# A gated attention and MLP block on one core: another order of the prelude

## The reference

```python
x = x + tanh(g_xattn[0]) * wkv(time_decay, time_first, layernorm(x), ctx)
x = x + tanh(g_ffn[0]) * ffn(layernorm(x), W1, W2, W3)

# ffn: D = 512, H = 2048
hidden = silu(x @ W1.T) * (x @ W3.T)
hidden = fwht(hidden)                 # orthonormal Walsh-Hadamard over H
out = hidden @ W2.T
```

## Time and profile before

| | |
|---|---|
| Median of three runs | 1129.24 us (1128.84 to 1130.64) |
| The profiled execution's own time | 1130.67 us |
| Its span, first to last instruction | 1128.8 us |
| PE busy | 1074.0 us, 95% of the span |
| DVE, ACT, POOL busy | 586.9, 305.3, 291.2 us |
| Mean granted clock of PE | 0.982 |

### The profile page before, as it was taken

One profiled execution on the slowest core, in us unless ns is written; L12 is line 12 of the kernel. 1 busy time (PEld: TensorE's weight loads), 2 busy tenths in 40 slices (PEclk: granted clock), 3 DMA queues, 4 the chain that ended last, 5 costly groups with the idle time before them and its releaser, 6 DMA issues.

```text
span 1128.8 us, 12951 instructions
## 1 busy us (share of the span) xinstructions
PE 1074.0 (95%) x4878; PEld 504.0 (45%) x4972; DVE 586.9 (52%) x849; ACT 305.3 (27%) x373; POOL 291.2 (26%) x194
## 2 busy tenths in 40 slices
PE   5677999799999999999999999999999999999998
PEld 2235444344444444444444444444444444444443
DVE  7744686537527555556527454556537464541112
ACT  5634542132312330231312330141412330110000
POOL 0121115212431134213431134213341225211111
PEclk9787999999999999999999999999999999999999
DMA  9924103000120012000120011000120000000001
GB/s 344 355 71 146 60 1 112 0 38 1 38 75 1 38 38 75 1 40 1 38 75 1 38 38 75 1 39 1 38 75 1 38 1 1 1 19 19 1 1 38
DMA packets 20387, 55.65 MB, mean 49 GB/s; under 512 B 1504, under 2 KB 10848, under 8 KB 17504
## 3 DMA queue, kind: packets, MB, share of 16 engines
q1 hardware_dynamic: 20320, 54.73, 13.6%
HBM read 42.14 MB, written 12.58 MB: 48 GB/s over the span
## 4 chain that ended last, share of the span: by engine, by line
PE 92%; ACT 3%; DVE 3%; issue 2%; DMA 1%; SPq 0%; DVEq 0%; ACTq 0%
PE pg L478 10%; PE pl L478 10%; PE po L486 10%; PE pg L476 10%; PE pl L476 10%; PE po L484 9%; PE pl L477 9%; PE pg L477 9%; PE po L485 9%; PE po L459 2%; PE po L452 1%; PE pst L411 1%; DMA w3h<-w_t 1%; ACT w L655 1%; PE pst L447 1%
## 5 line engine op out<-in xcount | busy, mean ns | idle before, releaser
L1053 POOL TENSOR_TENSOR work<-work 128x512 bf16<-128x512 f32 (+1 forms) x132 | 204.9, 1552 | 710.9 <-DVE work L903 710.9
L896 DVE TENSOR_TENSOR work<-work,pl 128x512 f32<-128x512 f32 (+1 forms) x132 | 88.3, 669 | 459.3 <-PE pl L478 446.3
L636 ACT ACTIVATE work<-pg 128x512 f32<-128x512 f32 (+1 forms) x132 | 77.1, 584 | 628.2 <-PE pg L478 628.2
L476 PE MATMUL pg<-xn,w1h 128*128 128x512 f16 (+1 forms) x528 | 198.7, 376 | 7.5 <-DVE xn L888 6.0
L478 PE MATMUL pg<-xn,w1l 128*128 128x512 f16 (+1 forms) x528 | 198.6, 376 | 2.0 <-issue 0.2
L478 PE MATMUL pl<-xn,w3l 128*128 128x512 f16 (+1 forms) x528 | 197.3, 374 | 1.4
L476 PE MATMUL pl<-xn,w3h 128*128 128x512 f16 (+1 forms) x528 | 197.3, 374 | 0.0
L486 PE MATMUL po<-work,w 128*128 128x512 f16 x512 | 194.0, 379 | 1.7
L484 PE MATMUL po<-work,w 128*128 128x512 f16 x512 | 194.1, 379 | 0.0
L477 PE MATMUL pl<-xn,w3h 128*128 128x512 bf16 (+1 forms) x502 | 187.4, 373 | 0.0
L477 PE MATMUL pg<-xn,w1h 128*128 128x512 bf16 (+1 forms) x493 | 185.2, 376 | 0.0
(11 more groups left out here) (134 smaller groups left out, 905.9 us busy)
## 6 DMA issues: line engine op xcount, KB each, us to landing
ev<-ctx_t SPq DMA_DIRECT2D x7, 1024.0 KB, 5.6
xin<-x_t SPq DMA_DIRECT2D x7, 1024.0 KB, 4.9
bv<-x_tok SPq DMA_DIRECT2D x7, 1024.0 KB, 8.2
out_t<-x SPq DMA_DIRECT2D x7, 1024.0 KB, 3.9
x<-w_t SPq DMA_DIRECT2D x6, 512.0 KB, 6.0
w_turn<-work SPq DMA_DIRECT2D x2, 1024.0 KB, 6.5
xn<-w_t SPq DMA_DIRECT2D x4, 512.0 KB, 6.1
psum<-w_t SPq DMA_DIRECT2D x3, 512.0 KB, 7.0
```

The costliest lines, as they stand in the source:

```text
L476: pe.matmul(bank[:, 0:run.n(j)], hi, nh, start=(k == 0), stop=False)
L636: act.activation(sg[:, j % 2, 0:run.n(j)], pg[:, 0:run.n(j)], ACT.Silu).then_inc(gated, 1)
L896: dve.tensor_tensor(hf[:, j % 2, run.cols(j)], sg[:, j % 2, 0:n], pl[:, j % 2, 0:n], ALU.mult).then_inc(hidden, 1)
L1053: pool.tensor_tensor(hl[:, j % HBUF, run.cols(j)], hf[:, j % 2, run.cols(j)], hh[:, j % HBUF, run.cols(j)], ALU.subtract).then_inc(hid_lo, 1)
```

## The change

It rewrites the order of the prelude on all five engines; no operation is computed another way. On PE, batch 0's `turn_x1` and `turn_xn` stand among the `mix_rows`, and turn into bank `pg` instead of a bank of `po`. Only three tiles of W2's second step stand ahead of `Run(0)`'s first slot; the other 13 stand one, three, three, three behind its four slots and three behind batch 1's `turn_xn`, all ahead of `ffn(b)`. Within these, PE's queue now has `mix_slots(i)`, `less_hi(i - 1)`, and ACT's `tile_hi(i)`, `tile_lo(i - 1)`. All `keep_rows` are ACT's. On DVE batch 0's second moments stand ahead of batch 1's denominator, and batch 1's `over` ahead of the first product of slot 0. POOL takes the constants that DVE made. SP issues batch 1's tokens, both halves of the context and units 0 and 1 earlier. `FIRST_AT` has most steps one or two slots earlier, and unit 5 moves into slot 0 of `ffn(b)`, with the later units spread in another way.

```diff
-FIRST_AT = dict(tok=3, tok_norm=3, exps=((4, 0), (4, 2), (5, 0), (5, 2)), weigh=6, scan_b=7, den=8, log=8, scan_a=9,
+FIRST_AT = dict(tok=2, tok_norm=2, exps=((4, 0), (4, 2), (5, 0), (5, 2)), weigh=6, scan_b=6, den=7, log=7, scan_a=7,
...
-        turn_banks = (pst[:, :], po[:, KT - 1, :])
+        turn_banks = ((pst[:, :], pg[:, :]), (pst[:, :], po[:, KT - 1, :]))
...
-        unit_slot = {0: (6, 7), 1: (8,), 2: (9,), 3: (10,), 4: (11,), 5: (12,), 6: (13,), 7: (14,), 8: (15,)}
+        unit_slot = {0: (5,), 1: (6,), 2: (7, 8), 3: (9,), 4: (10, 11), 5: (12,), 6: (13,), 7: (14,), 8: (15,)}
...
+            load_half_tokens(1)
             load_rows(0)
-            load_half_tokens(1)
             load_half_v(0)
             load_rows(1)
+            load_half_v(1)
             load_rows(2)
-            load_half_v(1)
+            load_half_x(0)
             load_rows(3)
-            load_half_x(0)
+            for n in range(2):
+                load_unit(n)
             put_rows(0)
-            load_unit(0)
+            load_half_x(1)
             put_rows(1)
             turn_rows(0)
-            load_unit(1)
             put_rows(2)
             turn_rows(1)
-            load_half_x(1)
             put_rows(3)
             turn_rows(2)
-            load_unit(2)
-            load_unit(3)
+            for n in range(2, 4):
+                load_unit(n)
             turn_rows(3)
-            for n in range(4, 8):
+            for n in range(4, 6):
                 load_unit(n)
             load_v(1)
+            for n in range(6, 10):
+                load_unit(n)
             load_x(1)
-            for n in range(8, 11):
-                load_unit(n)
+            load_unit(10)
...
+
+            def ahead(run, j):
+                ups(run, j)
+                up(run, j, w3h, w3l, pl[:, j % 2, :], hidden, 2, lin)
...
-            for i in range(2):
-                mix_rows(i)
+            mix_rows(0)
             for m in range(2):
                 transposes(a, m)
-            for i in range(2, 8):
+            for i in range(1, 4):
                 mix_rows(i)
             for m in range(2):
                 transposes(b, m)
-            for i in range(8, TILES):
+            for i in range(4, 10):
                 mix_rows(i)
+            turn_x1(0)
+            for i in range(10, TILES):
+                mix_rows(i)
+            turn_xn(0)
             for i in range(3):
-                mix_slots(i)
-            turn_x1(0)
-            for i in range(3, 5):
-                less_hi(i - 3)
-                mix_slots(i)
-            turn_xn(0)
-            for i in range(5, 8):
-                less_hi(i - 3)
                 mix_slots(i)
             pe.wait_ge(xn_hi, 2)
             pe.wait_ge(xn_lo, 2)
-            for j in range(LATE_PAIRS):
-                if j < AHEAD:
-                    ups(a, j)
-                    up(a, j, w3h, w3l, pl[:, j % 2, :], hidden, 2, lin)
-                for i in range(8 + 2 * j, 10 + 2 * j):
-                    less_hi(i - 3)
-                    mix_slots(i)
+            ahead(a, 0)
+            less_hi(0)
+            less_hi(1)
+            mix_slots(3)
+            less_hi(2)
+            ahead(a, 1)
+            for i in range(4, 7):
+                mix_slots(i)
+                less_hi(i - 1)
             turn_x1(1)
-            for i in range(TILES - 3, TILES):
-                less_hi(i)
+            ahead(a, 2)
+            for i in range(7, 10):
+                mix_slots(i)
+                less_hi(i - 1)
+            ahead(a, 3)
+            for i in range(10, 13):
+                mix_slots(i)
+                less_hi(i - 1)
             turn_xn(1)
+            for i in range(13, TILES):
+                mix_slots(i)
+                less_hi(i - 1)
+            less_hi(TILES - 1)
             ffn(b)
...
+            keep_rows(0)
             act.wait_ge(biases, 1)
             for m in range(2):
                 exps(a, m)
             act.wait_ge(limited, 1)
             act.activation(weight, tfc, ACT.Exp).then_inc(cst_weight, 1)
             tok_normalise(b)
-            for i in range(4, 7):
+            for i in range(1, 4):
                 keep_rows(i)
             for m in range(2):
                 exps(b, m)
-            for i in range(7, 9):
-                keep_rows(i)
             logs(a)
             inverses(a)
-            for i in range(9, TILES):
-                keep_rows(i)
             for n in range(2):
                 unit_hi(n)
+            for i in range(4, 14):
+                keep_rows(i)
+            x1_normalise(0)
+            for i in range(14, TILES):
+                keep_rows(i)
+            turned_hi(0)
+            logs(b)
+            inverses(b)
+            act.wait_ge(put[0], 16)
+            silu(a, 0)
             for i in range(3):
                 tile_hi(i)
-            logs(b)
-            inverses(b)
             tile_lo(0)
-            x1_normalise(0)
+            tile_lo(1)
             tile_hi(3)
-            tile_lo(1)
-            turned_hi(0)
-            tile_hi(4)
+            tile_lo(2)
             for n in range(2, 4):
                 unit_hi(n)
-            for i in range(2, 5):
-                tile_lo(i)
-                tile_hi(i + 3)
-            act.wait_ge(put[0], 16)
-            for j in range(LATE_PAIRS):
-                if j < AHEAD:
-                    silu(a, j)
-                for i in range(5 + 2 * j, 7 + 2 * j):
-                    tile_lo(i)
-                    tile_hi(i + 3)
-                if j in (2, 3):
-                    unit_hi(j + 2)
+            silu(a, 1)
+            for i in range(4, 7):
+                tile_hi(i)
+                tile_lo(i - 1)
+            silu(a, 2)
+            for i in range(7, 10):
+                tile_hi(i)
+                tile_lo(i - 1)
+            unit_hi(4)
+            silu(a, 3)
+            for i in range(10, 13):
+                tile_hi(i)
+                tile_lo(i - 1)
             x1_normalise(1)
-            for i in range(TILES - 3, TILES):
-                tile_lo(i)
             turned_hi(1)
+            for i in range(13, TILES):
+                tile_hi(i)
+                tile_lo(i - 1)
...
+            tok_moments_of(b)
...
-                keep_rows(i)
             weigh(a)
             scan(a, ea, eb, scan_b)
...
             residual(a)
             scan(b, ea, eb, scan_b)
+            x1_moments_of(0)
             with_token(b, ea, eb, scan_b, den_done)
-            x1_moments_of(0)
             unit_lo(0)
             unit_lo(1)
             turned_lo(0)
             scan(b, v, bv, scan_a)
+            with_token(b, v, bv, scan_a, num_done)
+            over(b)
             dve.wait_ge(put[0], 16)
             dve.wait_ge(put[1], 16)
             times_lin(a, 0)
             hidden_hi(a, 0)
-            with_token(b, v, bv, scan_a, num_done)
             unit_lo(2)
+            residual(b)
             times_lin(a, 1)
             hidden_hi(a, 1)
             unit_lo(3)
-            over(b)
-            residual(b)
+            x1_moments_of(1)
             times_lin(a, 2)
             hidden_hi(a, 2)
             unit_lo(4)
             times_lin(a, 3)
             hidden_hi(a, 3)
-            x1_moments_of(1)
-            unit_lo(5)
             turned_lo(1)
             ffn(b)
...
-            for i in range(8):
+            pool.memset(ones[:, :], 1.0 / D).then_inc(ones_set, 1)
+            pool.memset(decays[:, :, 0:2], 0.0).then_inc(pads_set, 1)
+            pool.wait_ge(mats_loaded, 16)
+            pool.tensor_scalar(minus[:, :], ident, -1.0, None, ALU.mult).then_inc(minus_set, 1)
+            pool.wait_ge(cst_decay, 1)
+            pool.tensor_copy(decays[:, :, 2:ROW],
+                             decay.unsqueeze(2).to_broadcast([P, KT, T - 1])).then_inc(rows_decay, 1)
+            for i in range(5):
                 tile_clamp(i)
             pool.wait_ge(put[1], 16)
-            for j in range(LATE_PAIRS):
-                for i in range(8 + 2 * j, 10 + 2 * j):
-                    tile_clamp(i)
-                if j < AHEAD:
-                    hidden_lo(Run(0), j)
+            hidden_lo(Run(0), 0)
+            for i in range(5, 8):
+                tile_clamp(i)
+            hidden_lo(Run(0), 1)
+            for i in range(8, 10):
+                tile_clamp(i)
+            hidden_lo(Run(0), 2)
+            for i in range(10, 13):
+                tile_clamp(i)
+            hidden_lo(Run(0), 3)
```

More of the change, by code:

```diff
@@ L52 @@
                sum_var=12, var=(13, 0), rsqrt=13, norm=14)
-FIRST_AT = dict(tok=3, tok_norm=3, exps=((4, 0), (4, 2), (5, 0), (5, 2)), weigh=6, scan_b=7, den=8, log=8, scan_a=9,
-                inv=9, num=10, quot=10, over=11, resid=11, sum_mean=11, mean=(12, 1), centre=12, square=12,
-                sum_var=13, var=(14, 0), rsqrt=14, norm=15)
+FIRST_AT = dict(tok=2, tok_norm=2, exps=((4, 0), (4, 2), (5, 0), (5, 2)), weigh=6, scan_b=6, den=7, log=7, scan_a=7,
```

(30 more changed lines are left out.)

21 lines of the change are left out of this document (6 added, 15 removed).

## The result

The changed kernel took 1103.38 us (median of 4, 1102.97 to 1104.28), the kernel before 1129.94 (median of 4): ratio 0.9766, 95% interval 0.9749 to 0.9783. It is 26.6 us faster; 1099 was forecast, and the range held it. The profiled execution after took 1102.97 us with a span of 1101.1 (before 1130.67 and 1128.8), and I compare these two.

What follows compares the result with a forecast made beforehand. PE, busy in the full runs, could gain only before them: prelude order, `ffn(b)`'s cold start, next chunk's norm. 1130.7 - 18.5 - 2.6 - 0.7 - 8.5 = 1100.4, median 1099; forecast 1095 to 1105, range 1090 to 1112.

Steps and rivals of the forecast that it cites:

- the 2.0 for units: Prelude, before batch 1's turn and slot 2: a wait of 2.0 us for units 2 and 3.
- the 1.7 for a cold slot 0: Prelude: 1.7 us added for a cold stretch at the start of slot 0.
- Part 1: Prelude up to `Run(0)`: first scan at 17.4 us, first slot at 45.0 instead of 62.35.
- Part 2: Prelude from `Run(0)`'s first slot to `ffn(b)`, which starts at 84 us, 18.5 us earlier.
- the walk's 82.3: Start of `ffn(b)` in us as walked step by step, before the addition for a cold stretch.
- Part 3: `ffn(b)`: cold start gone -2.6, slot 4's wait -0.7, next chunk's norm wait and its low clock -8.5 us.
- The first rival: The prelude runs cold, slots at 5.1 us instead of 2.6: about 1110 us; 12 in 100.
- two signs: Clock of 1.00 from `Run(0)`'s first slot to the end; ACT waiting for unit 3 between 50 and 57 us.
- (2): The second chunk's front doesn't catch up, its norm misses slot 14 and 8.5 us stay: 1107; 10 in 100.
- (3): Prelude not bounded by its order but by turns or loads, `ffn(b)`'s gain alone won: 1118 to 1120; 8 in 100.
- (4): Slower: W2's quarters come late in SP's queue, behind turns and puts, and tile 12 waits: 1134; 3 in 100.
- (5): Better than walked, with no wait for units: 1093; 10 in 100.

Runs made afterwards that it cites:

- Experiment 1: Changed kernel with W2's first quarter loaded ahead of batch 1's tokens again, as before the change: 1100.75 us.
- Experiment 8: Changed kernel with DVE starting batch 1's quotient only when POOL has clamped tiles 0 to 2: 1101.37 us.
- experiment 9: Kernel of 1097.28 us (first quarter first, second norm early, three tiles before batch 1's reciprocals), with SiLU 0 also before those reciprocals: 1098.26 us.
- experiment 5: Changed kernel with batch 1's second norm before SiLU 3, its turn back right behind slot 3, tiles 10 to 15 in one piece: 1100.93 us.
- Experiment 2: Changed kernel with the old slot table of the first full run (FIRST_AT): 1112.4 us.
- experiment 3: Kernel before the change with only the new slot table of the first full run (FIRST_AT): 1123.71 us.
- experiment 4: Changed kernel with the old order of the tiles' two steps on PE and ACT, their places between slots kept: 1119.15 us.
- experiment 6: Changed kernel with three tile_hi and two tile_lo ahead of batch 1's reciprocals on ACT, less_hi 0 and 1 before slot 0: 1102.2 us.

## Why the prediction was right

The sum was 1100.4 for the profiled execution, which took 1102.97. The 2.6 us stand at two places, both ahead of `ffn(b)`, partly offset by a third. That the forecast came this near is in part luck. Two terms of the walk never came as they stood, the 2.0 for units and the 1.7 for a cold slot 0. Without them it would have given `ffn(b)` at 80 and a median of 1095, 8 us too early instead of 4.

- **Part 1, off by 1.6.** I let the scan start at 17.4 since fewer instructions stood ahead of `weigh` on DVE and PE. It started at 19.57, and slot 0 at 46.57 instead of 45.0. The failed step is what PE itself waits for first: the change issues batch 1's tokens ahead of W2's first quarter, which landed at 13.5, and my walk had moved PE's work without the transfer under it. Experiment 1 gives its price, 2.6 us, by putting the load back. Slot 0 then came 1.0 sooner than walked, so the rest of this part was a little too long and hid some of the error.
- **Part 2, slot 0 to slot 1: 10.7 us, where 6.7 were in the walk.** ACT began the reciprocals at 44.7, not 41.5, and had SiLU 0 done at 51.1, not 48.2; 1.6 of these 2.9 us are part 1's and 1.3 are new. From there to slot 1 it took 6.1 us, not 3.5: the clamps took 1.44, 1.58 and 0.69 instead of 0.61, and behind PE's wait of 3.83 the clock was 0.50, so that one mixing took 1.91 instead of 1.02. The failed term is the round trip of the first tiles, priced with POOL undisturbed. Experiment 8 shows the clamps' part, 1.4 us, and 9 that ACT's work would have bounded soon behind it.
- **Part 2, the rest.** The wait of 2.0 for units 2 and 3 didn't happen: units 2 and 3 landed at 55.8 and 57.1, and with slot 1 itself late ACT read them only at 58.04 and 58.99. So slot 1 to slot 2 took 8.2 instead of 9.4, though slot 1 took 3.3 us instead of 2.6. Three tiles took 3.84 (3.9 forecast), slot 2 to slot 3 6.5 (6.5), slot 3 to `ffn(b)` 15.0 (14.7), with a wait of 2.3 for the second norm inside, which experiment 5 removed. With the walk's 82.3: + 1.6 + 4.0 - 1.2 + 0.3 = 87.0, measured 86.9. The 1.7 that I had added for a cold stretch had the right kind of cause and the wrong place: slot 0 ran at full clock, and the clock was low at slot 1 and the tile ahead of it, behind another wait.
- **Part 3: -12.1, forecast -11.8.** No cold start of `ffn(b)` (2.6), 0.86 instead of 1.9 at slot 4, no norm wait (6.0) and full clock at the chunk's change (2.5). PE waits at slot 4 for SiLU 3, which stands behind ACT's normalising, and no longer for the transposes. Experiment 2 carries the table's part, 9.0 where 8.5 + 0.7 were forecast; on the old prelude, in experiment 3, it was less.
- **The first rival and the clock.** The cold prelude (1) came true for a short stretch. From slot 0 on, the clock was low only from 53 to 58.5 us, behind the wait of 3.83; everywhere else the mixing took 1.02, the full clock's time, also between slots. So two signs were not met: a clock of 1.00 to the end held from 58.5 on and not from slot 0, and ACT never waited for unit 3. Ahead of slot 0 it was 0.50 from 28 to 36 behind a wait of 5.40, as the walk had it. The Trainium skill's rule (TensorE: Matmul & The Clock Gate, HAM oscillation) says that gaps between short bursts throttle the array again; the trace agrees behind the wait of 3.83. Shorter waits went either way. With about 1 us before each mixing, experiment 4 ran at 0.97 from 69 to 91, but tile 6 before that at 0.50. A wait of 2.30 left the clock full in the changed kernel, and in experiment 6 it was 0.57 behind the same wait. What decides stays open.
- **The other rivals.** The front caught up (2), and no wait of PE names a product. The order did bound (3): experiment 4 loses 15.8 us by order alone. The turns were never waited for (4). The better case (5) did not come, and its 1093 had no term behind it: without the wait for units the walk gives 1097, without the cold stretch too 1095.
- **Two slips that moved nothing.** The steps listed for DVE in slots 6 to 9 add up to 35.3 us, not 36.8, and half of a fully cold prelude puts `ffn(b)` at 93.5, not 95.

## What to carry to other kernels

When an edit moves compute earlier, walk the first DMA of its chain as well: one load of half its size put ahead of it in the same queue cost the whole chain 2.6 us. Software-pipelining a round trip over three engines (mix i + 1, then correct i) was worth 15.8 us against the other order, more than that order's 11.8 us of waits, since the clock also stayed up. Before reordering one queue further, add up its work in the stretch: experiment 9 moved a slot by 4 us, needed one table load more, and gained nothing.
